# A graph and expert kernel: where the first stage puts the norm's sums, its reciprocals and the ranking steps

## The reference

```python
def _layernorm(x, axis=-1, eps=1e-05):
    m = jnp.mean(x, axis=axis, keepdims=True)
    v = jnp.var(x, axis=axis, keepdims=True)
    return (x - m) / jnp.sqrt(v + eps)

def _L0_gnn_ref(x, W1, b1, W2, b2, edge_index):
    dst = edge_index[0]
    nbr = edge_index[1]
    agg = jax.ops.segment_sum(x[nbr], dst, num_segments=n)
    cnt = jax.ops.segment_sum(jnp.ones((nbr.shape[0],), x.dtype), dst, num_segments=n)
    mean = agg / jnp.maximum(cnt, 1.0)[:, None]
    return x @ W1.T + b1 + mean @ W2.T + b2

edge_index = jnp.stack([src, dst])
x = x + _L0_gnn_ref(_layernorm(x, axis=-1), ..., edge_index)
x = x + _L0_ffn_ref(_layernorm(x, axis=-1)[None], ...)[0]
```

## Time and profile before

| | |
|---|---|
| median of 3 runs | 2184.97 us (2181.34 to 2185.63) |
| the profiled execution's own time | 2197.56 us |
| its span | 2195.8 us |
| first gather (L496) starts | 137.04 us |
| first matmul of the second stage (L1007) starts | 144.71 us |
| busy in the whole span | PE 1847.6 (84%), DVE 1024.1 (47%), ACT 856.6 (39%), POOL 1213.8 (55%) |
| mean granted TensorE clock | 0.913 |

### The profile page before, as it was taken

How to read it: one execution, slowest core, us unless ns; L and a number is a source line. 1 busy time by engine, 2 the same in 40 slices (tenths; PEclk the granted TensorE clock), 3 DMA queues, 4 the chain that set the end, 5 groups by cost and what they waited for, 6 DMA issues and landing times.

```text
span 2195.8 us, 39738 instructions
## 1 busy us (share of the span) xinstructions
PE 1847.6 (84%) x10759; PEld 1546.8 (70%) x10759; DVE 1024.1 (47%) x2219; ACT 856.6 (39%) x2473; POOL 1213.8 (55%) x1146
## 2 busy tenths in 40 slices
PE   5867887789877678877777687599999999999998
PEld 3655665567645456656665576499999999999997
DVE  5767875878647666644343357611111111111111
ACT  4521561147511155522111255444444444444443
POOL 2036666677767677766676652154444545445453
PEclk9988999889989899988988777799999999999999
DMA  5122223222333322333332254324243342433421
GB/s 169 64 80 81 86 80 87 82 85 83 89 87 89 88 88 87 89 89 89 91 92 87 84 168 153 118 36 117 38 114 86 67 116 36 115 79 75 115 36 18
DMA packets 98488, 193.92 MB, mean 88 GB/s; under 512 B 25096, under 2 KB 65554, under 8 KB 94284
## 3 DMA queue, kind: packets, MB, share of 16 engines
q0 software_dynamic: 61376, 129.59, 23.5%
q1 hardware_dynamic: 25600, 52.03, 7.1%
q10 hardware_dynamic: 11404, 10.99, 1.5%
HBM read 361.33 MB, written 33.19 MB: 180 GB/s over the span
## 4 chain that ended last, share of the span: by engine, by line
PE 71%; DVE 11%; issue 7%; another core or an unknown queue 5%; ACT 2%; DMA 1%; POOL 1%; DVEq 1%; POOLq 0%; ACTq 0%; SPq 0%
PE bank L1007 22%; PE bank L1059 17%; PE bank L1071 17%; PE bank L821 6%; DVE agg L1578 2%; PE bank L917 2%; PE bank L875 2%; PE bank L1049 1%; POOL arena L496 1%; PE bank L951 1%; DVE arena L1133 1%; DVE arena L1195 1%; DVE arena L1202 1%; DVE arena L1164 1%
## 5 line engine op out<-in xcount | busy, mean ns | idle before, releaser
L496 POOL DMA_INDIRECT arena<-ytab,arena x784 | 819.5, 1045 | 382.4 <-issue 206.2
L1007 PE MATMUL bank<-arena 128*128 x2356 | 675.2, 426 | 67.9 <-issue 26.9
L1007 PEld LDWEIGHTS bank<-arena 128*128 128x128 f32 x2356 | 473.7, 213 | 166.5 <-issue 100.4
L732 ACT ACTIVATE arena<-bank,agg 128x128 f32<-128x128 f32 x848 | 311.8, 368 | 421.9 <-PE bank L1059 346.3
L1578 DVE TENSOR_TENSOR agg<-agg,bank 128x257 f32 x589 | 247.9, 421 | 417.1 <-PE bank L1007 226.2
L1059 PEld LDWEIGHTS bank<-arena,agg 128*128 128x128 f32 x3392 | 397.6, 193 | 6.3 <-DVE arena L1665 0.9
L1059 PE MATMUL bank<-arena,agg 128*128 128x128 f32 x3392 | 398.2, 276 | 0.5 <-DVE arena L1665 0.5
L1071 PE MATMUL bank<-agg,arena 128*128 128x256 f32 x1696 | 383.6, 379 | 0.0
L606 ACT ACTIVATE arena<-arena 128x1024 f32<-128x1024 f16 x148 | 156.3, 1056 | 571.3 <-DVE arena L1366 423.5
L526 POOL DMA_INDIRECT out<-arena x106 | 171.1, 1614 | 327.2 <-issue 266.1
L1071 PEld LDWEIGHTS bank<-agg,arena 128*128 128x128 f32 x1696 | 314.0, 190 | 38.3
(11 more groups left out here) (223 smaller groups left out, 1438.0 us busy)
## 6 DMA issues: line engine op xcount, KB each, us to landing
agg<-in_w SPq DMA_DIRECT2D x212, 1024.0 KB
agg<-in_b SPq DMA_DIRECT2D x106, 128.0 KB
arena<-ytab,arena POOLq DMA_INDIRECT x784
ytab<-arena SPq DMA_DIRECT2D x12, 512.0 KB, 2.9
node<-in_x SPq DMA_DIRECT2D x6, 896.0 KB, 12.4
out<-node ACTq DMA_DIRECT2D x6, 896.0 KB
xtab<-xn ACTq DMA_DIRECT2D x35, 128.0 KB
xtab<-xn SPq DMA_DIRECT2D x14, 128.0 KB
```

Source lines behind the costliest of these rows:

```text
L496: pool.indirect_dma_start(out=rows[:, v % RU, h, 0:D], out_offset=None, in_=ytab[:, :], in_offset=bass.IndirectOffsetOnAxis(ap=rowidx[g % ...
L732: act.activation(hT[:, m, :], bank[1 + m % 4][:, 0:T], ACT.Relu, bias=b1b[:, b, m:m + 1]).then_inc(s_fr, 1)
L1007: mm = pe.matmul(bank[n % NPS][:, 0:W], onehot[n // QUAD % 2][:, n % QUAD, h, :], pair[:, h * W:(h + 1) * W], start=(h == 0), stop=(h == H ...
```

## The change

In VectorE's list, `sums(3)` and `reciprocals(1)` stand ahead of the rank loop. Inside it, `sums(4)` to `sums(6)` stand in slots 1, 3 and 5 (before: `sums(3)` to `sums(5)` in slots 1, 4 and 7, `sums(6)` behind `positions(0)`), and `reciprocals(2)` to `(4)` in slots 2, 4 and 7 (before: `(1)` in slot 1, `(2)` and `(3)` in slots 4 and 8, `(4)` behind `segment_steps`). `reciprocals(5)` stands behind `segment_steps(0)`, `reciprocals(6)` behind place tile 6. In TensorE's list the nine rank parts are spread over 24 blocks (t = 10, 13, 15, 18, 21, 23, 26, 29 and 31), and `segment_blocks(0)` stands behind block 33, just ahead of the first placing. No instruction is added or dropped.

```diff
             for t in range(NT + 1):
                 y_part(t)
-                for r in share((8, 26), RT[0] + 1, t):
+                for r in share((8, 32), RT[0] + 1, t):
                     rank_part(0, r)
-                if t == 29:
+                if t == 33:
                     segment_blocks(0)
...
             step(v.tensor_tensor(val2_2[0:EP], twice(t_, slice(0, EC)), twice(s_, slice(0, EC)), ALU.add))
+            sums(3)
+            reciprocals(1)
             for t in range(RT[0] + 1):
                 rank_slot(0, t)
...
-                if t == 1:
-                    reciprocals(1)
-                if t in (1, 4, 7):
-                    sums(3 + (1, 4, 7).index(t))
-                if t in (4, 8):
-                    reciprocals(2 + (4, 8).index(t))
+                if t in (1, 3, 5):
+                    sums(4 + (1, 3, 5).index(t))
+                if t in (2, 4, 7):
+                    reciprocals(2 + (2, 4, 7).index(t))
             positions(0)
-            sums(6)
             segment_steps(0)
             settle()
-            reciprocals(4)
+            reciprocals(5)
             for i in range(PT[0]):
                 place_tile(0, i)
                 if i == 1:
                     segment_units(0)
-                if i in (3, 6):
-                    reciprocals((3, 6).index(i) + 5)
+                if i == 6:
+                    reciprocals(6)
```

## The result

The changed kernel takes 2176.77 us (median of 7 runs, 2172.09 to 2185.93); the kernel before, in 7 runs on the same chip, takes 2185.63 (2181.34 to 2189.72). The medians differ by 8.9 us. The ratio on record is 0.9948, interval 0.9929 to 0.9967: a gain of 11.4 us, between 7 and 15.5. It is larger than the seven and seven times give (0.996); with the two single executions of the kernel before that stand elsewhere in this text, 2197.56 and 2197.65 us, their means give 0.9949. Either way the gain is clear of zero and small. The forecast was 2170.5 with a range of 2166.0 to 2177.5. The direction holds and the time lies in the range, at its upper end. In the table further down, one of the twelve runs of c1 is left out: at 2087.61 us, with a mean granted clock of 0.894 against 0.949 to 0.957 in the others, it was in a slower state.

A forecast was written before the change was run, and what follows sets the result against it. First-stage placing was taken as VectorE-bound, its start delayed by waits for reciprocals. Rank part 7 at 71.6 us plus 47.3 of VectorE gives 118.9 against 133.4, 14.5 us earlier: 2184.97 - 14.5 = 2170.5 us, range 2166.0 to 2177.5.

The forecast's parts named there:

- What bounds the kernel, and the mechanism: End of first stage: 14 VectorE-bound place tiles, 35.1 us, start late because TensorE waits through keep_y for rstd, 12.7 us.
- Reciprocals in time: VectorE's list: reciprocals(1) done at 38.1 us, margin 1.0; reciprocals(2) at 50.7, margin 1.3; all stalls on rstd go.
- rival B: ScalarE's wait for rstd: one group, most likely 2, still stalls; gain 8.5 us, 2176.5 us; chance 8%.
- TensorE to rank part 7: TensorE's first-stage path: rank part 7 starts at 71.6 us, ends of the estimate 71.6 to 73.0.
- clock 1.00 from 31 to 78: Sign for the forecast: TensorE's granted clock at full from 31 to 78 us.
- the 19 blocks: TensorE from 42.9 us to rank part 7: five runs of three at 3.82 (else 4.1), two of two; 28.7 us.
- VectorE from there: VectorE from the start of rank part 7 to its last place tile: 47.3 us, ending at 118.9 us.
- the clash: GpSimd's clearing of agg lengthens L1211 in segment_steps; moving sums(6) takes 1.4 us off, 3.36 to 2.0.
- TensorE keeps up: First placing: segment_blocks behind block 33 costs nothing; TensorE places tile 0 by 82.2 us, VectorE asks at 84.2.
- Rival A: First places: TensorE's waits of 1.3 and 2.0 us bring half clock; gain 11.5 us, 2173.5 us; chance 11%.
- Rival C: First stage: stalls stay, only spreading rank parts acts; VectorE ends 5.9 us later, 2190.9 us; chance 3%.
- The median: Whole kernel: the first-stage shift of 14.5 us taken over whole, 2184.97 - 14.5 = 2170.5 us; forecast chance 70%.

The follow-up runs named there:

- c1: Control: the kernel before with one register operation more ahead of TensorE's and SyncE's register waits from the second stage on; 2058.28 us on chip 2, ratio 0.9993.
- e1: The changed kernel with c1's operation, rank parts back at every second block (8 to 26), segment_blocks at block 29; 2046.96 us on chip 2, ratio 0.9936.
- c2: Control: the changed kernel with c1's register operation; 2044.59 us on chip 2, ratio 0.9927.
- c4: Repeat of c2, the changed kernel with c1's register operation; 2045.83 us on chip 3, ratio 0.9940.
- e4: The changed kernel with c1's operation and sums(6) back behind positions(0); 2185.82 us in one run on chip 1.
- e5: e4 with GpSimd clearing all of agg ahead of the first mean; 2187.21 us in one run on chip 1.
- e3: The changed kernel with c1's operation and segment_blocks back behind block 29, rank parts still spread; 2189.34 us in one run on chip 1.
- e2: e1 with reciprocals(4) to (6) moved later, placing over blocks 30 to 49 and segment_bounds at block 34; 2040.75 us on chip 2, ratio 0.9909.
- e7: e2 with placing over blocks 33 to 49 and segment_bounds at block 36, as in the changed kernel; 2045.72 us on chip 3, ratio 0.9943.
- c3: Repeat of c1, the kernel before with the added register operation; 2057.89 us on chip 3, ratio 1.0001.

## Why the prediction held, and where it was off

- **What bounds the kernel, and the mechanism.** Held. In every trace with the new list no wait for `rstd` is over 0.5 us, e1 alone gives all of the gain, and the medians of the two repeats (13.7 and 12.1 us) show the shift whole at the end.
- **Reciprocals in time.** Held: `reciprocals(1)` done at 37.84 (38.1 said), `reciprocals(2)` at 51.07 (50.7 said), no stall of any group; rival B did not come.
- **TensorE to rank part 7: 73.22, 71.6 said.** This is the mis-sized term: 1.6 us late, past even the upper end that was given for it (73.0), in two halves. The first, 0.8, was there before the ranks began: the block behind rank part 0 starts at 43.70, 42.9 said, though the part itself took the predicted 2.3. In this execution TensorE came to full clock later (granted 0.50 from 29 to 31 us and 0.85 from 31 to 33; the kernel before had 0.66 and 1.00), so the sign "clock 1.00 from 31 to 78" was missed in its first 2 us. c2 repeats it (0.50 and 0.80, rank part 0 at 41.51). The windows from 29 to 31 us, of the changed kernel and of its repeat c4:

```profile
29.00:31.00 2.00, 2.00 (x7) 1.62 (x6) 2.00 (x2) 1.10 (x5) 0.54 (x1) 0.50 0.59 181
```

```profile
29.00:31.00 2.00, 1.57 (x9) 1.16 (x7) 1.97 (x3) 1.45 (x6) 1.09 (x2) 0.95 0.61 200
```

In c4 rank part 0 starts at 40.48, close to the 40.6 that the sum had, against 41.42; c4 then lost as much again at 0.82 and 0.87 between 39 and 50 us. The second, 0.8, is the 19 blocks: 29.5 us instead of 28.7. Three of the five runs of three blocks took 3.86, as chosen (3.82). Two took 4.19, just the other bound (4.1), those in which ScalarE also takes a group's root (L567). ScalarE's timeline of the changed kernel:

```profile
54.11 0.30 ACT L567 ACTIVATE std<-square,eps 128x7 f32<-128x7 f32 x1
...
65.81 0.30 ACT L567 ACTIVATE std<-square,eps 128x7 f32<-128x7 f32 x1
```

The text chose one value for all five; three were of one kind and two of the other.
- **VectorE from there: 47.8 us, 47.3 said.** By terms: to the read 0.61 (0.6), read 2.18 (2.06), `positions` 1.45 (1.44), `segment_steps` and reciprocal 2.03 (2.0), tiles 0 and 1 4.75 (4.76), `segment_units` 1.61 (1.7), 14 tiles 35.14 (34.7). Only the last is off, by 0.4: a wait of 0.65 for TensorE stands in it. (The last tile of the kernel before ends at 133.46 by its row, 132.78 + 0.68, where the prediction added 0.60; the shift is the same to a tenth.)
- **L1211.** Held, and shown by e4 and e5. That the clash could go over to the preparations in slot 0 was also foreseen: L1333 took 1.94, and its slack hid it (the preparations end at 41.06, VectorE then idles 2.73 us until the ranks at 43.80).
- **TensorE keeps up.** Held: waits of 1.29 and 1.86, 1.3 and 2.0 said, clock 1.00 behind them. Rival A did not come, in c2 and c4 neither (1.00 from 80 to 95 us). In e4 and e5, where TensorE had idled more ahead of the first places, the clock did fall (0.52 and 0.50 from 85 to 90 us). Moving `segment_blocks` cost nothing, as said; what the text left out is that its old place would have cost 5.8 us (e3).
- **Rival C was no program.** "The stalls stay and only the spreading acts" was priced at 2190.9 as if one could have it. With the old list of VectorE and the ranks from block 10 on, TensorE's block 10 waits for `keep_y` of block 7, that for `reciprocals(1)`, that stands behind the read of rank part 0, and that behind block 10 on TensorE: a circle. This is read off the lists; no run has it. The price says nothing; the one side on which the change could lose was a stall at `segment_blocks` or at the roots, as e3 has it.
- **The median.** Off by 6.3 us: 2.0 are the first gather (12.5 instead of 14.5 us earlier). The median of before with seven runs is 0.7 higher than with three. The other 3.6 are the shift of 12.5 in the two profiles against 8.9 between the two medians. The interval of the gain (7 to 15.5) contains 12.5, and the repeats gave 13.7 and 12.1 by the medians, so they are put down to the spread of medians; no run splits them further.

The part that the prediction didn't see is the coupling from ScalarE back to VectorE: a reciprocal early in the list also waits for its root. It cost nothing here because the ranks were spread, and 7.9 us of VectorE's time in e1.

## What to carry over

In engines with lists in order, look at where a small instruction stands, not at what it costs: 0.2 us of reciprocal behind a read that waited for another engine held 12.7 us of work. Put it forward together with what feeds it, and then read the list once more in the other direction, since what is early can now wait itself (e1, e3). Work that is moved out of one instruction's way can land on another's (e5): look at what runs beside its new place. When one engine has been made early, give the next one its work early too (e2 against e7), and look at how far the same stage of the same kernel repeats before trusting a difference of a few microseconds.

## What was not expected of the hardware

- The gather stages differ between chips by 140 to 142 us for the kernel before (1276.7 us against 1134.7 and 1136.3) and by 131 to 133 for the changed kernel (1268.7 against 1137.7 and 1135.4), while the first stage and the feed-forward part (781.4 to 782.8 everywhere) do not. GpSimd's idle time at the gathers is 382.4 us before on the first chip and 243.9 on the second.
- The granted clock behind the same gap is not the same from one execution to the next: after 3.1 us it was 0.69 in c1 and 1.00 in c3, which ran on another chip. In e4 gaps of 2.48, 0.47 and 1.37 us were followed by 0.52, while in the changed kernel gaps of 1.29, 0.27 and 1.86 were not followed by any fall.
- Only some VectorE instructions are held up by a clearing on GpSimd. TENSOR_SCALAR operations that read and write in SBUF grew by 1.4 to 2.3 us: 0.28 to 1.76 us (L1218 of e4), 0.58 to 2.03 us (L1331 of e4, on int32), and 0.58 to 2.83 beside clearings one behind the other (L1317 of e5). TENSOR_TENSOR of 125x400 and TENSOR_REDUCE of 125x800 kept their 0.57 and 0.99 us beside the same clearing. The TENSOR_TENSORs also read `bank` in PSUM, so for them kind and place are not told apart; the TENSOR_REDUCE works in `arena` alone.
- It goes the other way too. In the changed kernel a clearing starts at 38.32, while the TENSOR_SCALAR of 38.20 is still running; that one keeps its 0.57 us and the clearing takes 1.98 us instead of 1.59 (GpSimd's timeline):

```profile
38.32 1.98 POOL L481 MEMSET agg<- 128x1792 f32 x1
```
